# The null keys of the first wide attention: weights in token layout, and a second pair of matmuls once a sequence

## The chip, the cores and the metric

The kernel runs on one NeuronCore of a Trainium2 chip. The time is device microseconds, the median of three executions. A core has TensorE (PE, with its weight loads shown as PEld), VectorE (DVE), ScalarE (ACT), GpSimd (POOL) and SyncE (SP, which issues DMAs). Each works off its own instruction queue in order; they wait for each other by semaphores.

## What is computed

Four transformer layers in a row on 16 sequences of 256 tokens and 128 features, in float32. The change touches the first layer's attention only, with 16 heads of 64, ALiBi, a causal mask, normalized queries and keys, and two learned null keys and null values per head that every token sees:

```python
nkv = null_kv.reshape(HEADS, NUM_NULL_KV, 2, DIM_HEAD)
k = jnp.concatenate([nk, k], axis=2)        # nk, nv: the two null keys and values of each head
v = jnp.concatenate([nv, v], axis=2)
q = _l2norm(q) * q_scale
k = _l2norm(k) * k_scale
sim = jnp.einsum('bhid,bhjd->bhij', q, k) * ATTN_SCALE + alibi, causal mask
attn = jax.nn.softmax(sim, axis=-1)
out = jnp.einsum('bhij,bhjd->bhid', attn, v)
return out.transpose(0, 2, 1, 3).reshape(b, n, HEADS * DIM_HEAD) @ w_out
```

The input of the attention is normalized twice (a layer norm outside, one inside), so each sequence needs two means and inverse deviations for each half of 128 tokens. The result is added to `x`, which stays in SBUF as `XR` through the whole kernel.

## The kernel before

Eight stages run one after the other; each is a class with one method per engine (`pe`, `act`, `dve`, `pool`, `sp`). The first, `Wide` with `kind == 0`, is the first attention. Its work is cut into **units** of one sequence `b` and four heads `u`, 64 in all, numbered g = 4b + u, and one **prep** per sequence (layer norms, transpose of the tokens `zT`, scores of the null keys `sn`). A unit has 23 parts k = 0 to 22, a prep 9. The function `ticks` lays them on a common time line: a unit begins every 4 ticks, so in one tick five or six units are at parts that differ by 4. Within a tick the parts are sorted by `rank`; parts of equal rank stand in the order in which they began, older ones first. This list, `self.order`, is the queue of PE, ScalarE and VectorE; GpSimd has its own, `pool_order`, sorted by `pool_rank`, which here is the same.

The parts of a unit (`self.tk`): `qk` (k = 0, 1), queries and keys in token layout by three fp32r matmuls each (`mm3`, high and low halves); ScalarE squares (`sqr`) and copies (`raw`) them; VectorE sums the squares (`ss`, k = 1, 2); GpSimd takes the power -0.5 and scales `raw` (k = 3, semaphore `unitq`); PE turns them (`turn`, k = 6, 7), VectorE makes the low halves `QL` and `KL`; `mx` (k = 9, 10), row maxima of the scores, which PE computes two units ahead together with `st`; `v` (12); `mT` (15), the maxima `nm` transposed; `st` (17, 18), transposed scores, exponentiated by ScalarE into `P`; `pv` (20), weighted values and the sums `sm`; `sT` (21), the sums transposed and inverted (`rs`); `out` (22), the output product `Y` in two PSUM tiles, scaled by VectorE into `T` and added to `XR` by GpSimd in four operations (`pool_sum`).

PSUM has eight banks that the stage takes in turn (`self.G`, `K.ps.take`): who takes a bank waits until its former content has been read. The score part takes its four banks before its first instruction, the masks (`mk`).

The null keys, before: VectorE computes their scores and biases with four small operations and a reduction (`dve_null`, line 820 on, at k = 8). ScalarE exponentiates them (line 626), GpSimd lays the weights, split in a high and a low half, into `pn` (lines 925 to 928, k = 12). PE transposes both halves of `pn` in `mT` behind the `nm` transposes, ScalarE copies them out as `pnT` (line 634), and `pe_pv` starts its accumulation with two matmuls against `nvs` (null values) and one against `nvo` (ones, for the sums). `dve_nvs` builds both from three loads through the staging buffers before the first unit.

The inverse deviations (`pool_rstd`, two GpSimd operations for each of two halves) are made in the tick of the part that needs the statistics: prep k = 0 and k = 2; VectorE makes `z` in k = 2 and k = 4, PE turns it at k = 6.

The lines at which the rows below stand are those of the helpers where a helper records: 2578 to 2580 are `mm3`, 2583 is `acc`, 2586 is `tr` (transpose), 2592 and 2594 the statistics, 2599 and 2601 `pool_rstd`, 2607 `z`, 891 `pool_sum`, 912 the power and 917 the scaling of `raw`.

## Time and profile before

| | us |
|---|---|
| median of 3 runs | 2607.7 (2597.29 to 2611.27) |
| the profiled execution | 2604.87 |
| its span | 2603.1 |
| first wide attention, from the first `nm` transposes to the last sum | 65.6 to 839.7 |

In the lines of the time line each row is a start in us, a duration in us, the engine, the line of the kernel, the operation, output and inputs, and a count where like instructions were merged; a row of the windows has its length and then the busy us (and instructions) of PE, PEld, DVE, ACT and POOL, the granted clock, the DMA share and GB/s; in square brackets stands how long the engine had nothing to do before it and who ended that. A matmul's duration includes its way through the array, so the distance from one start to the next tells what it costs PE.

### The profile page before, as it was taken

Reading aid. Unit: us, or ns where it says so; the run is one execution under the profiler, and the core shown is the slowest. Engines: PE = TensorE matmul, PEld = TensorE weight load, DVE = VectorE, ACT = ScalarE, POOL = GpSimd, SP = SyncE. Lnnn points to the kernel's source line nnn. Section 1 sums busy time; section 2 is a strip of 40 time slices with the busy share of each in tenths; the row PEclk is TensorE's granted clock in tenths of the full one; section 3 lists DMA queues with packets and bytes.
Section 4 is the critical chain, followed back from the end, with each engine's and each line's share of the span. In section 5 each row is a group of like instructions: output and inputs, shape, how many; then the busy total and the mean of one; then the engine's idle time right before and its main releaser. Section 6 shows DMA issues by size and latency. Waiting matters only on the chain. (4 is left out here: it accounts for less than half of the span.)

```text
span 2603.1 us, 62284 instructions
## 1 busy us (share of the span) xinstructions
PE 2382.6 (92%) x23977; PEld 1851.5 (71%) x23977; DVE 1684.1 (65%) x4424; ACT 1477.2 (57%) x3068; POOL 1575.3 (61%) x2498
## 2 busy tenths in 40 slices
PE   3999999999999879988999999999999958788897
PEld 3888888888887546656777787777778747455555
DVE  4677777777675357774544467777777622577676
ACT  3666666666665457765444466666666523466665
POOL 4678777777785354443433267777777721666664
PEclk9999999999999979999999999999999979899999
DMA  5960000000000010000000000000000045000000
GB/s 201 328 209 2 2 2 2 2 2 2 2 2 2 1 45 2 2 2 12 21 1 1 3 2 6 6 6 4 6 6 5 5 124 184 17 10 8 8 4 33
DMA packets 23111, 83.10 MB, mean 32 GB/s; under 512 B 4097, under 2 KB 11010, under 8 KB 21794
## 3 DMA queue, kind: packets, MB, share of 16 engines
q1 hardware_dynamic: 19666, 71.90, 8.6%
q0 software_dynamic: 3152, 7.21, 0.9%
q8 instruction: 193, 3.16, 0.5%
q14 instruction: 100, 0.82, 0.1%
HBM read 71.89 MB, written 46.79 MB: 46 GB/s over the span
## 5 line engine op out<-in xcount | busy, mean ns | idle before, releaser
L891 POOL TENSOR_TENSOR XR<-XR,T 128x256 f32<-128x256 f32 x512 | 376.5, 735 | 152.9 <-DVE T L770 122.7
L645 ACT ACTIVATE P<-ps 128x384 f32<-128x384 f32 (+1 forms) x512 | 250.6, 541 | 180.0 <-PE ps L2583 178.6
L2583 PE MATMUL ps<-P,V 128*64 128x256 f32 (+3 forms) x4096 | 332.8, 346 | 9.9 <-DVE O L1377 7.9
L1361 DVE TENSOR_REDUCE bm<-ps 128x3 f32<-128x384 f32 x512 | 260.2, 550 | 110.5 <-PE ps L2583 109.5
L2583 PEld LDWEIGHTS ps<-P,V 128*64 128x64 f32 (+1 forms) x4096 | 185.7, 123 | 131.0 <-issue 34.3
L1296 ACT ACTIVATE P<-ps 128x768 f32<-128x768 f32 x256 | 207.7, 811 | 97.6 <-PE ps L2583 96.7
L781 DVE TENSOR_REDUCE sm<-ps 128x2 f32<-128x512 f32 (+1 forms) x256 | 130.8, 553 | 181.0 <-PE ps L2583 180.9
L1461 POOL TENSOR_SCALAR_AFFINE_SELECT P<-P 128x512 f32<-128x512 f32 x256 | 162.6, 635 | 119.2 <-ACT P L1296 116.5
L904 POOL TENSOR_TENSOR PS<-P 128x256 f32<-128x256 f32 x256 | 181.6, 735 | 70.5 <-ACT P L645 70.1
L2583 PE MATMUL ps<-mk,identb 128*128 128x256 bf16 (+1 forms) x1024 | 204.9, 293 | 14.4 <-DVE bm L1361 12.2
L912 POOL TENSOR_TENSOR ss<-ss,nhalf 128x16 f32<-128x16 f32 x64 | 187.7, 2933 | 5.3
L770 DVE TENSOR_TENSOR T<-ps,rs 128x512 f32<-128x512 f32 x256 | 163.9, 682 | 9.7 <-PE ps L2583 8.3
L2578 PE MATMUL ps<-wA,zT 128*128 128x256 f32 (+1 forms) x544 | 168.9, 311 | 1.3 <-issue 1.3
L2583 PE MATMUL ps<-QH,KH 64*128 64x256 f32 (+1 forms) x1024 | 163.1, 314 | 1.0 <-ACT MT L632 0.9
L757 DVE TENSOR_REDUCE nm<-ps 128x2 fp32r<-128x512 f32 x256 | 161.9, 676 | 2.6 <-PE ps L2583 2.6
L653 ACT ACTIVATE OT<-ps 128x512 f32<-128x512 f32 x128 | 76.5, 598 | 153.0 <-PE ps L2583 153.0
L2601 POOL TENSOR_TENSOR stat<-stat,nhalf 128x1 f32<-128x1 f32 x256 | 147.2, 575 | 21.3
L2579 PE MATMUL ps<-wA,zT 128*128 128x256 f32 (+1 forms) x544 | 154.1, 284 | 0.0
L1668 POOL TENSOR_TENSOR hr<-hf,hr 128x512 fp32r<-128x512 f32 x48 | 62.0, 1292 | 150.5 <-DVE hr L1657 138.5
L2580 PE MATMUL ps<-wA,zT 128*128 128x256 f32 (+1 forms) x544 | 153.0, 282 | 0.0
L2583 PE MATMUL ps<-QH,KL 64*128 64x256 f32 (+1 forms) x1024 | 144.9, 279 | 0.0
L2583 PE MATMUL ps<-MT,KB 64*128 64x256 f32 (+1 forms) x1024 | 144.7, 278 | 0.0
(309 smaller groups left out, 7007.3 us busy)
## 6 DMA issues: line engine op xcount, KB each, us to landing
rows_i<-in_zero SPq DMA_DIRECT2D x16, 1208.0 KB, 31.2
rows_o<-in_zero SPq DMA_DIRECT2D x16, 1208.0 KB, 80.6
w<-in_m_w SPq DMA_DIRECT2D x23, 578.0 KB, 4.0
zt<-rows_i SPq DMA_DIRECT2D x23, 128.0 KB, 3.3
rows_o<-yo POOLq DMA_DIRECT2D x23, 128.0 KB, 3.9
stg<-in_t_w SPq DMA_DIRECT2D x11, 256.0 KB, 2.7
XR<-in_x SPq DMA_DIRECT2D x4, 512.0 KB, 8.6
out<-XR SPq DMA_DIRECT2D x8, 256.0 KB, 2.0
```

The costliest lines, as they stand in the source:

```text
L645: e.activation(self.P[at % 6][:, :], K.ps.ap("st", s, g, h)[:, 0:self.w], ACT.Exp, bias=0.0, scale=1.0 if kind == 0 else 0.125).then_inc(K ...
L757: e.tensor_reduce(nm[:, :, 64 * par + n], ps[:, :].rearrange("p (t c) -> p t c", t=2), X, ALU.max, negate=True).then_inc(K.ps.out_of("mx", ...
L770: e.tensor_tensor(self.T[g % 2][:, par], K.ps.ap("Y", s, g, par)[:, :].rearrange("p (a t c) -> p a t c", a=2, t=2), r[:, par].unsqueeze(3) ...
L891: p = po.e.tensor_tensor(x, x, self.T[g % 2][:, par, pr], ALU.add)
L904: po.e.tensor_tensor(self.PS[g % 2][:, h, :], P[:, 0:256], P[:, 256:512], ALU.add).then_inc(self.halved, 1)
L912: d = po.step(e.tensor_tensor(ss[:, 32:48], ss[:, 16:32], K.nhalf[:, 0:16], ALU.pow))
L1296: e.activation(self.P[(2 * g + n) % 6][:, :, 0:384], K.ps.ap("st", s, g, n)[:, :, 0:384], ACT.Exp, bias=0.0, scale=self.scale).then_inc(K. ...
L1361: e.tensor_reduce(bm[:, h, :], K.ps.ap("mx", s, g, h)[:, 0:384].rearrange("p (a c) -> p a c", c=128), X, ALU.max, negate=True).then_inc(K. ...
L1461: e.affine_select(own, own, [[0, 4], [1, 128]], ALU.is_ge, 0.0, base=0, channel_multiplier=-1).then_inc(self.masked, 1)
L2578: self.te.matmul(o, L[0], R[0], start=start, stop=False)
L2579: self.te.matmul(o, L[1], R[0], start=False, stop=False)
L2583: return self.te.matmul(o, l, r, start=start, stop=True, skip_group_check=True)
```

## The change

Three things change in this stage.

1. The null keys' weights stay in token layout. GpSimd makes the scores (`pool_null`, two operations behind the norm at k = 3), VectorE keeps only the reduction of `dve_null`. GpSimd adds the two weights of each head (k = 12, `pnull`); VectorE adds this to the transposed sums ahead of the reciprocal. At k = 22 GpSimd multiplies the weights by `rs` into a `pn` of [128, 64] for the whole sequence (`shared`). The transposes of `pn` in `mT` and the three matmuls ahead of `pv` are gone.
2. Once a sequence a new item "null" with two parts: PE transposes `pn`, ScalarE copies it out; PE multiplies it by `nvw` (null values times the output weights, [64, 256]), ScalarE copies the result out as `ny`, GpSimd adds it to `XR` (`nulled`). Its ranks are 3 and 0.5, its GpSimd rank is 8. `nvw` is made once by eight fp32 matmuls (`pe_nvw`) and two ScalarE copies at k = 8 of the first unit, from one load, which replaces the three loads and `dve_nvs`. The stage is done when the last `nulled` is counted.
3. Order: GpSimd makes the deviations one part later (k = 1, 3) with rank 6, behind the unit work of the tick, and `pool_sum` one part later (k = 23, rank 7). VectorE gets its own order, `dve_order`, in which prep parts other than the transpose have rank 6. A unit has 24 parts.

```diff
@@ -139,7 +139,7 @@
         self.K, self.s, self.kind = K, s, kind
         self.causal = kind == 0
         if kind == 0:
-            first, last, unit = 8, 9, 23
+            first, last, unit = 8, 9, 24
             self.tk = {"qk": 0, "turn": 6, "mx": 9, "v": 12, "mT": 15, "st": 17, "pv": 20, "sT": 21, "out": 22}
...
+            if kind == 0:
+                items.append((16 * b + first + 12 + unit, 2, "null", (b,), 2))
...
+        self.dve_order = [w for w in ticks(items, self.dve_rank) if not self.is_early(*w)]
...
+        return (self.nulled, b + 1) if self.kind == 0 else (self.summed, 4 * b + 4)
...
+        if name == "null":
+            return 3 if k == 0 else 0.5
         if name != "unit":
             return 5 if name == "behind" else 1
...
         if self.kind == 2 and name == "unit":
             return 0 if self.part("st", k - 1) is not None else 2
+        if name == "unit" and k == self.tk["out"] + 1:
+            return 7
+        if name == "null":
+            return 8
+        if self.kind == 0 and name == "prep":
+            return 6
         return self.rank(name, k)
...
+    def dve_rank(self, name, k):
+
+        return 6 if self.kind == 0 and name == "prep" and k != self.zT_at else self.rank(name, k)
...
+            elif name == "null":
+                self.pe_null(pe, *a, k)
             elif name == "unit":
+                if self.kind == 0 and a == (0, 0) and k == 8:
+                    self.pe_nvw(pe)
                 self.pe_unit(pe, *a, k)
+
+    def pe_nvw(self, pe):
+
+        K, n = self.K, self.nvs_at
+        ps = K.ps.take(pe, self.G, "nvw")
+        K.staged(pe, n)
+        for j in range(8):
+            p = pe.e.matmul(ps[0:64, 0:128], K.stg[n % 2][:, 64 * j:64 * j + 64], K.wO[:, 128 * j:128 * j + 128],
+                            start=j == 0, stop=j == 7)
+        p.then_inc(K.ps.full_of("nvw"), 1)
+
+    def pe_null(self, pe, b, k):
+
+        K, s = self.K, self.s
+        if k == 0:
+            ps = K.ps.take(pe, self.G, "pnT", s, b)
+            pe.wait_ge(self.shared, 4 * b + 4)
+            K.tr(ps[0:64, 0:128], self.pn[b % 2][:, :]).then_inc(K.ps.full_of("pnT", s, b), 1)
+        if k == 1:
+            ps = K.ps.take(pe, self.G, "nul", s, b)
+            pe.wait_ge(self.nvs_in, 1)
+            pe.wait_ge(*K.ps.read("nvw"))
+            pe.wait_ge(*K.ps.read("pnT", s, b))
+            K.acc(ps[:, 0:256], self.pnT[b % 2][:, :], self.nvw[:, :], start=True).then_inc(K.ps.full_of("nul", s, b), 1)
 
...
@@ -373,10 +420,6 @@
                     pe.wait_ge(*K.ps.read("mx", s, g, h))
             for i in range(2):
                 p = K.tr(ps[:, 128 * i:128 * i + 128], fv(nm[:, i, :]))
-            if kind == 0:
-                pe.wait_ge(self.pnull, g + 1)
-                for i in range(2):
-                    p = K.tr(ps[0:96, 256 + 128 * i:384 + 128 * i], fv(self.pn[g % 2][:, i, :]))
             p.then_inc(K.ps.full_of("mT", s, g), 1)
...
-        if kind == 0:
-            pe.wait_ge(self.nvs_in, 4)
-            pe.wait_ge(*K.ps.read("mT", s, g))
-            for pr in range(2):
-                c = 256 * u + 128 * pr
-                K.acc(pv[:, 256 * pr:256 * pr + 256], self.nvs[:, 0, c:c + 128], self.pnT[g % 2][:, :], start=pr == 0)
-            K.acc(sm[:, 0:256], self.nvo[:, 4 * u:4 * u + 4, :].rearrange("p h c -> p (h c)"), self.pnT[g % 2][:, :],
-                  start=True)
         pe.wait_ge(*K.ps.read("v", s, g))
...
-                              P[2 * pr + par][:, c:c + w], start=kind == 2 and kt == 0 and pr == 0)
+                              P[2 * pr + par][:, c:c + w], start=kt == 0 and pr == 0)
...
-                    p = K.acc(sm[32 * h:32 * h + 32, q:q + w], self.one[:, 0:32], P[h][:, c:c + w])
+                    p = K.acc(sm[32 * h:32 * h + 32, q:q + w], self.one[:, 0:32], P[h][:, c:c + w], start=kt == 0)
...
+            elif name == "null":
+                if k == 0:
+                    b = a[0]
+                    if b >= 2:
+                        ac.wait_ge(*self.K.ps.filled("nul", self.s, b - 2))
+                    ac.wait_ge(*self.K.ps.filled("pnT", self.s, b))
+                    ac.e.activation(self.pnT[b % 2][:, :], self.K.ps.ap("pnT", self.s, b)[0:64, 0:128], ACT.Copy).then_inc(
+                        self.K.ps.out_of("pnT", self.s, b), 1)
+                if k == 1:
+                    b = a[0]
+                    if b >= 2:
+                        ac.wait_ge(self.nulled, b - 1)
+                    ac.wait_ge(*self.K.ps.filled("nul", self.s, b))
+                    ac.e.activation(self.ny[b % 2][:, :], self.K.ps.ap("nul", self.s, b)[:, 0:256], ACT.Copy).then_inc(
+                        self.K.ps.out_of("nul", self.s, b), 1)
             elif name == "unit":
                 if a == (0, 0) and k == 2:
                     self.act_kb(ac)
+                if self.kind == 0 and a == (0, 0) and k == 8:
+                    self.act_nvw(ac)
...
+    def act_nvw(self, ac):
+
+        K = self.K
+        ac.wait_ge(self.nv_zero, 1)
+        ac.wait_ge(*K.ps.filled("nvw"))
+        for t in range(2):
+            r = slice(32 * t, 32 * t + 32)
+            i = ac.e.activation(self.nvw[r, 128 * t:128 * t + 128], K.ps.ap("nvw")[r, 0:128], ACT.Copy)
+            i.then_inc(*((K.ps.out_of("nvw"), 1) if t else (self.nvs_in, 1)))
...
-            i = e.activation(self.MT[g % 2][:, :], ps[:, 0:256], ACT.Copy)
-            if kind == 0:
-                i = e.activation(self.pnT[g % 2][:, :], ps[0:96, 256:512], ACT.Copy)
-            i.then_inc(K.ps.out_of("mT", s, g), 1)
+            e.activation(self.MT[g % 2][:, :], ps[:, 0:256], ACT.Copy).then_inc(K.ps.out_of("mT", s, g), 1)
...
-        for name, a, k in self.order:
+        for name, a, k in self.dve_order:
...
-                if self.kind == 0 and a == (0, 0) and k == 0:
-                    self.dve_nvs(dv)
                 self.dve_unit(dv, *a, k)
...
         if self.part("sT", k) is not None:
+            rs, sums = self.rs[g % 2], K.ps.ap("sT", s, g)[:, 0:256].rearrange("p (a c) -> p a c", c=32)[:, :, 0]
+            if kind == 0:
+                if g >= 2:
+                    dv.wait_ge(self.shared, g - 1)
+                dv.wait_ge(self.pnull, g + 1)
             dv.wait_ge(*K.ps.filled("sT", s, g))
-            e.reciprocal(self.rs[g % 2][:, :], K.ps.ap("sT", s, g)[:, 0:256].rearrange("p (a c) -> p a c", c=32)[:, :, 0]
-                         ).then_inc(K.ps.out_of("sT", s, g), 1)
+            if kind == 0:
+                dv.after(dv.step(e.tensor_tensor(rs[:, :], sums, self.sm[g % 4][:, 48:56], ALU.add)))
+            e.reciprocal(rs[:, :], rs[:, :] if kind == 0 else sums).then_inc(K.ps.out_of("sT", s, g), 1)
...
-    def dve_nvs(self, dv):
-
-        K, e, v = self.K, dv.e, self.nvs
-        for n, (a, b) in enumerate(((0, 512), (512, 1024), (1024, 1040))):
...
     def dve_null(self, dv, b, u):
 
 
-        K, s, g, e, ss, sm = self.K, self.s, 4 * b + u, dv.e, self.ss[(4 * b + u) % 4], self.sm[(4 * b + u) % 4]
-        rq = ss[:, 32:40].rearrange("p (t a r) -> p t r a", t=2, a=2).unsqueeze(4)
-        snr = self.sn[b % 2][:, :].rearrange("p (t h n) -> p t h n", t=2, n=2)[:, :, 4 * u:4 * u + 4, :].rearrange(
-            "p t (a r) n -> p t r a n", a=2)
-        sn = sm[:, 16:32].rearrange("p (t r a n) -> p t r a n", t=2, r=2, a=2)
-        nb = K.pc("nbias", 8 * u, 8).rearrange("p (a r n) -> p r a n", a=2, r=2)
-        dv.wait_ge(*K.ps.read("sn", s, b))
-        dv.wait_ge(self.unitq, 2 * g + 1)
-        if g >= 4:
-            dv.wait_ge(self.rec, g - 3)
-        for t in range(2):
-            d = dv.step(e.tensor_tensor(sn[:, t], snr[:, t], rq[:, t].to_broadcast([128, 2, 2, 2]), ALU.mult))
-        dv.after(d)
-        for t in range(2):
-            d = dv.step(e.tensor_tensor(sn[:, t], sn[:, t], nb, ALU.add))
-        dv.after(d)
+        g, e, sm = 4 * b + u, dv.e, self.sm[(4 * b + u) % 4]
+        dv.wait_ge(self.scored, g + 1)
         e.tensor_reduce(sm[:, 8:16], sm[:, 16:32].rearrange("p (a n) -> p a n", n=2), X, ALU.max, negate=True).then_inc(
             self.snl, 1)
...
         if self.kind == 0:
-            for pn in self.pn:
-                e.memset(fv(pn[:, :, :]), 0.0).then_inc(K.pn_in, 1)
+            e.memset(self.nvw[:, :], 0.0).then_inc(self.nv_zero, 1)
         for name, a, k in self.pool_order:
             if name == "prep":
                 n = K.nb[s] + (4 if self.kind == 0 else 2) * a[0]
-                if k == 0 or (k == 2 and self.kind == 0):
+                if self.kind == 0 and k in (1, 3) and not self.is_early(name, a, k - 1):
                     for i in range(2):
-                        K.pool_rstd(po, n + k + i)
+                        K.pool_rstd(po, n + k - 1 + i)
+                if self.kind == 2 and k == 0:
+                    for i in range(2):
+                        K.pool_rstd(po, n + i)
                 if k == 3 and self.kind == 2:
                     self.pool_bias(po, a[0])
...
+            elif name == "null" and k == 1:
+                b = a[0]
+                xs = K.XR[:, 2 * b:2 * b + 2, :].rearrange("p t c -> p (t c)")
+                po.wait_ge(self.summed, 4 * b + 4)
+                po.wait_ge(*K.ps.read("nul", s, b))
+                e.tensor_tensor(xs, xs, self.ny[b % 2][:, :], ALU.add).then_inc(self.nulled, 1)
             elif name == "unit":
                 if self.kind == 0:
                     self.pool_unit(po, 4 * a[0] + a[1], k)
                 elif self.part("st", k - 1) is not None:
                     self.pool_halves(po, 4 * a[0] + a[1], k - 1 - self.tk["st"])
-                if k == self.tk["out"] + (1 if self.kind == 2 else 0):
+                if k == self.tk["out"] + 1:
                     self.pool_sum(po, *a)
             elif name == "load":
...
+    def pool_null(self, po, g):
+
+        K, s, b, u, e, ss, sm = self.K, self.s, g // 4, g % 4, po.e, self.ss[g % 4], self.sm[g % 4]
+        rq = ss[:, 32:40].rearrange("p (t h) -> p t h", t=2).unsqueeze(3).to_broadcast([128, 2, 4, 2])
+        snr = self.sn[b % 2][:, :].rearrange("p (t h n) -> p t h n", t=2, n=2)[:, :, 4 * u:4 * u + 4, :]
+        sn = sm[:, 16:32].rearrange("p (t h n) -> p t h n", t=2, n=2)
+        nb = K.pc("nbias", 8 * u, 8).rearrange("p (h n) -> p h n", n=2).unsqueeze(1).to_broadcast([128, 2, 4, 2])
+        po.wait_ge(*K.ps.read("sn", s, b))
+        if g >= 4:
+            po.wait_ge(self.rec, g - 3)
+        po.after(po.step(e.tensor_tensor(sn, snr, rq, ALU.mult)))
+        e.tensor_tensor(sn, sn, nb, ALU.add).then_inc(self.scored, 1)
+
...
+            self.pool_null(po, g)
         if k == self.tk["mx"] + 3:
-            sm, pn = self.sm[g % 4], self.pn[g % 2]
+            sm = self.sm[g % 4]
             po.wait_ge(self.rec, g + 1)
-            if g >= 2:
-                po.wait_ge(*K.ps.filled("mT", s, g - 2))
-            po.wait_ge(K.pn_in, 2)
-            s6 = sm[:, 32:48].rearrange("p (t a) -> p t a", t=2)
-            d = po.step(e.tensor_copy(pn[:, :, 0:8], s6))
-            e.tensor_copy(pn[:, :, 64:72], s6)
-            po.after(d)
-            e.tensor_tensor(pn[:, :, 32:40], s6, fv(pn[:, :, 0:8]), ALU.subtract).then_inc(self.pnull, 1)
+            ex = sm[:, 32:48].rearrange("p (a n) -> p a n", n=2)
+            e.tensor_tensor(sm[:, 48:56], ex[:, :, 0], ex[:, :, 1], ALU.add).then_inc(self.pnull, 1)
+        if k == self.tk["out"]:
+            b, u = g // 4, g % 4
+            sm, ex = self.sm[g % 4], self.sm[g % 4][:, 32:48].rearrange("p (t h n) -> p t h n", t=2, n=2)
+            if b >= 2 and u == 0:
+                po.wait_ge(*K.ps.filled("pnT", s, b - 2))
+            po.wait_ge(*K.ps.read("sT", s, g))
+            e.tensor_tensor(
+                self.pn[b % 2][:, :].rearrange("p (t h n) -> p t h n", t=2, n=2)[:, :, 4 * u:4 * u + 4, :], ex,
+                self.rs[g % 2][:, :].rearrange("p (t h) -> p t h", t=2).unsqueeze(3).to_broadcast([128, 2, 4, 2]),
+                ALU.mult).then_inc(self.shared, 1)
...
-            for n, (a, b) in enumerate(((0, 512), (512, 1024), (1024, 1040))):
-                n += self.nvs_at
-                K.sp_stage(sp, n, K.stg[n % 2][0:96, 0:b - a], K.t["nvs"][:, a:b])
             for c in range(5):
                 n, w = self.kb_at + c, 512 if c < 4 else 128
                 K.sp_stage(sp, n, K.stg[n % 2][:, 0:w], K.t["kb0"][:, 512 * c:512 * c + w])
+            K.sp_stage(sp, self.nvs_at, K.stg[self.nvs_at % 2][:, :], K.t["nvs"])
```

## Rows read from the trace of the kernel before

**Rows 1.** The page, busy time of each engine, its share of the span, instructions.

```profile
PE 2382.6 (92%) x23977; PEld 1851.5 (71%) x23977; DVE 1684.1 (65%) x4424; ACT 1477.2 (57%) x3068; POOL 1575.3 (61%) x2498
```

**Rows 2.** The windows: one unit, one sequence; busy us of each engine, clock, DMA.

```profile
429.15:440.87 11.72, 11.72 (x142) 9.97 (x141) 8.66 (x25) 7.40 (x16) 9.63 (x15) 1.00 0.01 1
404.84:453.21 48.37, 48.37 (x567) 40.84 (x566) 34.95 (x91) 30.28 (x66) 37.72 (x53) 1.00 0.01 2
```

**Rows 3.** The waits of 62 to 880 us: total us, times, longest.

```profile
POOL XR L891 <- DVE T L770: 122.7, 49, 6.7
PEld ps L2586 <- POOL pn L928: 3.9, 16, 0.8
```

**Rows 4.** The time line of PE, from the second turn of a unit's inputs to its sums.

```profile
413.73 0.38 PE L2586 MATMUL ps<-ident,S 128*128 128x128 f32 x2
413.95 0.60 PE L2583 MATMUL ps<-mk,identb 128*128 128x256 bf16 x4
417.65 0.38 PE L2586 MATMUL ps<-ident,pn 128*96 128x128 f32 x2
417.87 0.60 PE L2586 MATMUL ps<-ident,raw 128*128 128x128 f32 x4
418.22 0.49 PE L2583 MATMUL ps<-pnT,nvs 96*128 96x256 f32 x2
418.55 0.28 PE L2583 MATMUL ps<-pnT,nvo 96*128 96x256 f32 x1
418.76 1.52 PE L2583 MATMUL ps<-P,V 128*64 128x256 f32 x16
```

**Rows 5.** The same time line, around a first half of `qk`, and ScalarE beside it.

```profile
422.39 0.28 PE L2580 MATMUL ps<-wA,zT 128*128 128x256 f32 x1
422.51 0.61 PE L2583 MATMUL ps<-mk,identb 128*128 128x256 bf16 x4
410.23 0.22 ACT L583 ACTIVATE sn<-ps 128x64 f32<-128x64 f32 x1
421.13 0.38 ACT L659 ACTIVATE S<-ps 128x256 f32<-128x256 f32 x1 [0.21 <-PE ps L2583]
...
422.76 0.60 ACT L596 ACTIVATE sqr<-ps 128x512 f32<-128x512 f32 x1 [0.17 <-PE ps L2580]
423.26 0.59 ACT L597 ACTIVATE raw<-ps 128x512 f32<-128x512 f32 x1
```

**Rows 6.** The time line of GpSimd in the same sequence.

```profile
430.59 3.17 POOL L891 TENSOR_TENSOR XR<-XR,T 128x256 f32<-128x256 f32 x4 [2.75 <-DVE T L770]
434.07 2.93 POOL L912 TENSOR_TENSOR ss<-ss,nhalf 128x16 f32<-128x16 f32 x1
437.08 2.05 POOL L917 TENSOR_TENSOR raw<-raw,ss 128x512 f32<-128x512 f32 x2
439.67 0.23 POOL L2599 TENSOR_SCALAR stat<-stat 128x1 f32<-128x1 f32 x1
440.86 0.57 POOL L2601 TENSOR_TENSOR stat<-stat,nhalf 128x1 f32<-128x1 f32 x1
```

**Rows 7.** The time line of VectorE, with one row of PE (446.06).

```profile
429.17 0.68 DVE L726 TENSOR_REDUCE ss<-sqr 128x8 f32<-128x512 f32 x1
441.54 0.35 DVE L2607 TENSOR_SCALAR z<-XR,stat 128x128 f32<-128x128 f32 x1 [0.32 <-POOL stat L2601]
445.17 0.74 DVE L734 SCALAR_TENSOR_TENSOR KL<-ps,par,KH 128x512 fp32r<-128x512 f32 x1
446.06 0.60 PE L2583 MATMUL ps<-mk,identb 128*128 128x256 bf16 x4
448.27 1.29 DVE L781 TENSOR_REDUCE sm<-ps 128x2 f32<-128x512 f32 x2 [0.45 <-PE ps L2583]
```

**Rows 8.** The time line at the start (PE) and at the end (GpSimd) of the stage.

```profile
64.71 1.09 PE L2586 MATMUL ps<-ident,raw 128*128 128x128 f32 x4 [2.51 <-POOL raw L917]
836.48 3.19 POOL L891 TENSOR_TENSOR XR<-XR,T 128x256 f32<-128x256 f32 x4 [1.67 <-DVE T L770]
```

51 lines of the change are left out of this document (20 added, 31 removed).

## The prediction

> **What bounds the kernel now.** I read the page first: TensorE is busy for 92% of the span, no other engine for more than 65% [rows 1]. The stretches of the first wide attention, second: four units (one sequence) take 48.37 us there, PE has no empty stretch, the granted clock is 1.00, and GpSimd is the next engine with 37.7 us, VectorE 35.0, ScalarE 30.3 [rows 2]. The waits, third: GpSimd's largest wait in this stage is for VectorE's `T` (122.7 us), and the only wait of PE's weight loads for another engine that recurs is the one for the null weights `pn`, 3.9 us in all [rows 3]. So the stage's length is what PE's queue issues; anything taken out of it counts 64 times, and any new wait of PE counts in full.
>
> An adjacency in the time line misleads here: a producer and a PE instruction that stand side by side often belong to different units. The null weights and maxima that PE transposes come from the unit's part several ticks back, so these have microseconds in hand. Where the slack is small has to be read from the order of the ticks.
>
> **What PE loses, per unit.** Two transposes of `pn` (417.65 to 417.87, 0.22 us) go. The two `nvs` matmuls and the `nvo` one run from 418.22 to the first `P,V` at 418.76, 0.54 us [rows 4]. With them gone the raw transposes, whose fourth starts three steps of 0.11 behind 417.87, at 418.20, are followed by `P,V` directly. The same kind of step, from a 128-column transpose to the next group, takes 0.11 us from the second transpose of `S` to the masks (413.73 to 413.95 for two) [rows 4]. I get 418.76 - 418.20 - 0.11 = 0.45, and 0.22 + 0.45 = 0.67. Lower bound: only the array time goes, two transposes at 0.11 and three matmuls of 256 columns at the 0.12 us that the last `wA,zT` takes to the masks [rows 5], 0.58; upper bound: the two stretches whole, 0.76. Times 64: 42.9 us (37 to 49). The wait for `pn` goes with them, 3.9 us [rows 3].
>
> The page "TensorE: Matmul & The Clock Gate" of the Trainium skill, section "Back-to-back issue gap", gives N/2.4 + 2.5 ns from one matmul to the next at the full clock. That is 0.11 us for 256 columns, which the trace bears out (0.12), but 0.056 for 128, where the transposes show 0.11. By the page alone the five instructions would be worth 0.44 us a unit, 28 us in all, and the forecast below would turn into 9 us slower than before.
>
> **What PE gains: the null pair.** Once a sequence PE transposes the four units' shares (rank 3: last in its tick, behind the `qk` matmuls of the newest unit) and then multiplies by `nvw` (rank 0.5: first in the next tick). Nothing stands between the two on PE, and between them ScalarE has to copy the transposed weights out; on ScalarE that copy is queued behind `sqr` and `raw` of the same `qk`. From the rows: last `qk` matmul starts at 422.39, masks at 422.51; ScalarE's second copy starts at 423.26 and its successor can start 0.5 later (as `raw` starts 0.5 after `sqr`), at 423.76 [rows 5]. A copy of 128 columns lies between the 64 columns of `sn` (0.22) and the 256 of `S` (0.38) [rows 5]: 0.28. So PE goes on at 424.1. The product is fp32 of 256 columns: `P,V` needs 1.52 us for sixteen passes, eight of 256 and eight of 128 side by side in pairs [rows 4], so 0.25 at most for one pass of 256; I take 0.46 for the two. The masks start at 424.56 instead of 422.51: 2.05 us. Bounds: 0.6 if the copy is hidden (transpose and product alone), 2.6 if the weight load of the product waits as well. All that is queued on PE behind it (scores, and through them both reductions) is late with it. Fourteen sequences have a `qk` in that tick, the last two have only the copy of V (about 1.3): 31.3 us.
>
> **GpSimd.** Per unit it loses three small operations and gets four (two for the null scores, one sum, one product), each taken at the 0.2 of the ones that go, plus the add of `ny` once a sequence at the 0.79 of one of the four parts of `XR` (3.17 for four) [rows 6]. Its sum falls from work behind a wait to work without one: `pool_sum` no longer sits at the tick in which `T` is made, where it idled 2.75 us [rows 6], but behind the next unit's norm. A unit is then 5.4 (norm) + 0.5 + 3.2 + 0.4 = 9.5 us, a sequence 38 + 3.5 (four deviations) + 0.8 = 42.3 against 47.9 of PE: 88%, not the bound. The norm's result has more time in hand than before.
>
> **The deviations and VectorE.** VectorE loses four small operations and gets one in front of the reciprocal; with 35 of 48 us it isn't the bound, this is worth nothing by itself. Its order decides. Let N be the start of the two `nm` transposes, 440.87 in the unit with the first norm. (a) `z` (k = 2) and its statistics now stand behind `QL` but still ahead of `KL`; the wait of 0.32 for the deviation goes, since GpSimd makes it two ticks earlier. `KL` ended at 445.91 and PE's masks, which take its bank, began at 446.06 [rows 7], 0.11 later than they would have by 0.12 from the last matmul. In the new kernel `KL` ends at N + 4.72, PE needs it at N + 4.41 (5.08 - 0.67), plus the 0.15 from VectorE to PE: a wait of 0.46, where it was 0.11. Added: 0.35, times 16 = 5.6 us (0 to 10). (b) `z` (k = 4) waits for deviations that GpSimd now makes behind the norm. The sum of squares ends at N + 0.7 (429.17 + 0.68 against 429.15 [rows 2, 7]), the power starts 0.35 later, the norm ends at N + 6.1 by the rows of 434.07 and 437.08, the null scores at 6.6, the two deviations (439.67 to 441.43 for two) at N + 7.5 and 8.4 [rows 6]. VectorE stands at `z` until N + 8.85 with the sums of squares, the first maxima and the reciprocal queued behind it. The first maxima were taken at 448.27, N + 7.4 [rows 7], and would now be ready at N + 7.0: 1.9 us late. Who waits: the eight banks go round, and these banks are taken next by the transposes of `z` and by `Y`, some 3.3 us of PE work later (PE runs scores, their maxima and the second half in between). The two maxima (1.29 [rows 7]) end at N + 10.1, PE wants the bank at about N + 10.4. I charge 0.1 a sequence, 1.6 us (0 to 26).
>
> **Start and end.** `nvw` is eight fp32 matmuls on PE before the first maxima; PE is starved by GpSimd there (it waits 2.51 us for `raw` at 64.7 [rows 8]), so this is hidden, but `z` of sequence 1 now waits for a deviation behind a norm: 1.3 us (-2 to 3). The removed conversion of `nvs` on VectorE was beside ScalarE's work: nothing. At the end GpSimd adds `ny` after the last sum (836.48, four in 3.19 us [rows 8]): 0.8. SP issues three transfers fewer and one more, all ahead of the large fills: nothing.
>
> **The sum**, against the profiled execution (2604.9 us; span 2603.1): -42.9 - 3.9 + 31.3 + 5.6 + 1.6 + 1.3 + 0.8 = -6.2, so 2598.7. The median of the runs shown is 2.8 above that execution (2607.7): forecast 2601 us, its own range 2592 to 2613.
>
> **Rivals.** *B, the null pair is hidden*: PE reaches the product when the weights are out, because ScalarE comes to them earlier than I read. For it: ScalarE is idle a third of the time. Against: every `sqr` waits for PE, so it is never ahead of it. Price: 14 x 1.45 = 20 us less, 2581. *C, only array time is saved*: the step from the transposes to `P,V` keeps the 0.21 that it has behind `nvo` (418.55 to 418.76 [rows 4]), so 0.58 a unit: 5.8 us more, 2607, no change. *D, the other side*: VectorE at `z` (k = 4). My slack there is 0.1 to 0.3 us; each microsecond by which GpSimd's deviations come later (its null scores with broadcast operands slower than 0.25 each, a norm that starts later) stands on PE once a sequence. With 1.6 us more it is 16 x 1.6 = 26 us, 2627; it decides against the change from 0.4 us on. For it: GpSimd is in nobody's shadow here, a chain of power, product and two deviations without a gap; against: the rest of VectorE's queue in that tick is short.
>
> **Chances.** Forecast 0.48, B 0.17, C 0.20, D 0.15. What one measurement can tell from no change is about 0.5%, 13 us. Faster by more: most of B and an edge of the forecast, 0.29; slower: most of D and an edge of C, 0.17; the same 0.54. The range 2579 to 2624 holds the forecast and C, and reaches to B's value and D's.
>
> **What would show it.** Three of four units at some 11.05 us between `nm` transposes, from 11.72. Once a sequence a PE wait of 1.5 us for ScalarE's `pnT` ahead of the product: if it is under 0.5, B. GpSimd's wait for `T` gone from first place. VectorE's `z` waiting 3 to 4 us for `stat` once a sequence, and a PE wait behind it: over 0.5 us is D. It is wrong if a sequence takes under 46.5 or over 49 us.

## The result: slower by 0.47%, and the page after

| | us |
|---|---|
| changed kernel, median of 10 runs | 2616.97 (2614.89 to 2624.24) |
| kernel before, beside it on the same chip, 10 runs | 2607.48 (2596.80 to 2612.61) |
| ratio to the kernel before, 95% interval | 1.0047 (1.0033 to 1.0062) |
| profiled execution and its span | 2624.24; 2622.6 (before 2604.87; 2603.1) |
| first wide attention, from the first to the last `nm` transposes | 67.2 to 834.5 (before 65.6 to 823.5) |

The forecast was 2601 us, 0.25% under the median shown before. The time lies in the range given (2579 to 2624), outside the forecast's own one (2592 to 2613), and the sign is wrong. The profiled execution is the longest of its ten: the stage with the change and what follows up to `beff` (the start of the second wide attention) take 13.6 us more than before (`beff` from 1478.3 to 1491.9 us), which is what the ratio says (0.47% is 12.2 us). The rest of its 19.5 us more arises in stages that the change doesn't touch. So 13.6 is the number to explain, against the -6.2 of the sum.

The page of the changed kernel, busy time and TensorE's granted clock in 40 slices; it answers to [rows 1]:

```profile
PE 2377.0 (91%) x23721; PEld 1833.5 (70%) x23721; DVE 1594.8 (61%) x4222; ACT 1471.5 (56%) x3038; POOL 1605.8 (61%) x2577
PEclk9999999999999969999999999999999979799999
```

256 instructions fewer on PE, 5.6 us less busy time, and yet slower: the page alone would have passed for a gain. The windows tell more. Here each row is one unit of the changed kernel, from its `nm` transposes to those of the next, two sequences one behind the other (columns as in [rows 2]: length, busy us of PE, PEld, DVE, ACT, POOL, granted clock, DMA):

```profile
348.60:360.87 12.27, 11.97 (x138) 9.69 (x137) 8.33 (x23) 7.62 (x16) 11.24 (x18) 1.00 0.01 2
360.87:372.69 11.82, 11.82 (x142) 10.05 (x141) 7.21 (x20) 7.36 (x16) 8.87 (x12) 1.00 0.01 1
372.69:386.09 13.40, 12.03 (x140) 9.74 (x139) 6.20 (x15) 7.68 (x17) 9.61 (x13) 1.00 0.01 1
386.09:397.25 11.16, 11.16 (x136) 9.39 (x135) 7.57 (x23) 7.15 (x15) 9.38 (x13) 1.00 0.01 2
...
421.70:436.62 14.92, 13.55 (x140) 11.17 (x139) 6.59 (x18) 7.68 (x17) 9.60 (x13) 0.89 0.00 1
```

The first unit holds the transposes of `z`, the second the projection for `sn`, the third the null pair, the fourth nothing extra. Before, the four took 12.34, 12.59, 11.72 and 11.72 (the last is the first line of [rows 2]). Three things are to be seen. The clean unit is 0.56 shorter, not 0.67. The third unit has 13.40 - 12.03 = 1.37 us in which PE is idle. And in the next sequence the same unit takes 14.92, with the same 1.37 us idle but 1.52 more busy for the same 140 matmuls, at a granted clock of 0.89 of full. Whole sequences, windows of the same kind:

```profile
348.60:397.25 48.65, 46.99 (x549) 38.86 (x548) 29.30 (x79) 29.81 (x64) 39.10 (x56) 1.00 0.01 2
...
496.45:546.64 50.19, 48.53 (x550) 40.31 (x549) 29.41 (x79) 29.81 (x64) 39.42 (x57) 0.97 0.01 2
546.64:595.28 48.64, 46.98 (x549) 38.85 (x548) 29.30 (x79) 29.80 (x64) 39.43 (x57) 1.00 0.01 2
```

From the third sequence on every second one shows the clock at 0.97 and 1.5 us more, six in all (they begin at 199, 298, 397, 496, 595 and 694 us). A sequence of 48.37 [rows 2] became one of 48.65 or of 50.2: even without the clock there would be no gain.

The time line of PE around the null pair, in the unit from 421.70 (it answers to [rows 5]; `pn` and `nvw` are the pair):

```profile
421.92 0.60 PE L2642 MATMUL ps<-ident,raw 128*128 128x128 f32 x4
422.45 1.52 PE L2639 MATMUL ps<-P,V 128*64 128x256 f32 x16
...
426.10 0.28 PE L2636 MATMUL ps<-wA,zT 128*128 128x256 f32 x1
426.21 0.27 PE L2642 MATMUL ps<-ident,pn 128*64 128x128 f32 x1
427.86 0.67 PE L2639 MATMUL ps<-nvw,pnT 64*128 64x256 f32 x2 [1.37 <-ACT pnT L587]
428.45 0.61 PE L2639 MATMUL ps<-mk,identb 128*128 128x256 bf16 x4
429.00 0.38 PE L2639 MATMUL ps<-QH,KH 64*128 64x256 f32 x2
...
432.06 0.41 PE L2636 MATMUL ps<-wA,zT 128*128 128x256 f32 x1
...
433.89 0.28 PE L2639 MATMUL ps<-QH,KL 64*128 64x256 f32 x2
```

From the last `qk` matmul to the masks it takes 2.35 us, where [rows 5] have 0.12: 2.23 for the pair. From 1.7 us behind the pause on, the same kind of matmul lasts 0.41 instead of 0.28 us and starts 0.21 instead of 0.12 behind its forerunner, until 433. The window of exactly that stretch is at half of the full clock, 1.2 GHz:

```profile
429.60:433.00 3.40, 3.40 (x27) 3.18 (x24) 1.43 (x3) 0.87 (x2) 2.59 (x5) 0.51 0.02 5
```

The waits of 62 to 890 us, those that answer to [rows 3] and the new ones (total us, times, longest):

```profile
POOL ss L963 <- DVE ss L783: 95.6, 44, 4.5
DVE z L2663 <- POOL stat L2657: 65.8, 45, 4.2
PE ps L2639 <- ACT pnT L587: 20.0, 16, 1.4
POOL XR L931 <- DVE T L833: 9.2, 5, 2.6
PEld ps L2639 <- DVE sm L844: 5.6, 14, 0.4
```

GpSimd's wait for `T` fell from 122.7 us to 9.2 and that of the weight loads for `pn` is gone. GpSimd now waits for its sums of squares, which come from PE by way of two engines; that is idle time of an engine that isn't the bound.

VectorE at the second `z` (with one row of GpSimd and three of PE), where rival D had its place, and `KL`; they answer to [rows 6, 7]:

```profile
451.70 0.72 DVE L791 SCALAR_TENSOR_TENSOR KL<-ps,par,KH 128x512 fp32r<-128x512 f32 x1
452.19 0.28 PE L2636 MATMUL ps<-wA,zT 128*128 128x256 f32 x1
452.57 0.60 PE L2639 MATMUL ps<-mk,identb 128*128 128x256 bf16 x4
...
455.65 0.34 DVE L2663 TENSOR_SCALAR z<-z,stat 128x128 f32<-128x128 f32 x1 [3.15 <-POOL stat L2657]
455.82 0.59 POOL L2657 TENSOR_TENSOR stat<-stat,nhalf 128x1 f32<-128x1 f32 x1
457.13 1.27 DVE L844 TENSOR_REDUCE sm<-ps 128x2 f32<-128x512 f32 x2
458.46 1.16 PE L2639 MATMUL ps<-wO,OT 64*128 64x128 f32 x16 [0.16 <-DVE sm L844]
```

### The profile page after: what moved, and what is told of

It reads as the page before. It is cut to its first block and busy times, and to the rows that moved or that the text cites. A ratio compares the mean times of both kernels' runs of the same rounds, so it can differ in the third digit from the quotient of the medians.

```text
span 2622.6 us, 61622 instructions
## 1 busy us (share of the span) xinstructions
PE 2377.0 (91%) x23721; PEld 1833.5 (70%) x23721; DVE 1594.8 (61%) x4222; ACT 1471.5 (56%) x3038; POOL 1605.8 (61%) x2577
## 5 line engine op out<-in xcount | busy, mean ns | idle before, releaser
L2634 PE MATMUL ps<-wA,zT 128*128 128x256 f32 (+1 forms) x544 | 171.3, 315 | 1.4 <-issue 1.3
L2635 PE MATMUL ps<-wA,zT 128*128 128x256 f32 (+1 forms) x544 | 155.4, 286 | 0.0
L2636 PE MATMUL ps<-wA,zT 128*128 128x256 f32 (+1 forms) x544 | 155.0, 285 | 0.0
L2639 PE MATMUL ps<-QL,KH 64*128 64x256 f32 (+1 forms) x1024 | 145.4, 279 | 0.0
```

Source lines behind the costliest of these rows:

```text
L2634: self.te.matmul(o, L[0], R[0], start=start, stop=False)
L2635: self.te.matmul(o, L[1], R[0], start=False, stop=False)
L2639: return self.te.matmul(o, l, r, start=start, stop=True, skip_group_check=True)
```

## The experiments

Two theories stood after the comparison. **Pause and clock**: the null pair leaves PE idle for 1.37 us, and this pause both costs its own length and brings the clock down behind it. **Late z** (D): the deviations behind the norm hold VectorE, and PE behind it. A third question was how much of the unit's saving is really there. All ratios are to the kernel before on the same chip; the changed kernel stands at 1.0047.

**e1, the product moved behind the work of its tick.** The only edit, in `rank`:

```diff
-            return 3 if k == 0 else 0.5
+            return 3 if k == 0 else 4
```

> The product with nvw keeps its tick but goes from the first to the last place in it (rank 4 instead of 0.5), on PE and ScalarE; GpSimd's order is untouched. Theory (the null pair leaves PE idle for about 1.4 us once a sequence, and every second time the granted clock falls to half for 3.4 us, which costs 1.5 us more): the wait for pnT goes from 20 us to under 1, no half-clock stretch is left between 240 and 740 us, and the kernel is 16 x 1.6 + 7 x 1.5 = 36 us faster than the changed kernel, about 2582 us, 1% under the kernel before. Rival (the stall is elsewhere given back, as in VectorE's z or in a bank that the pair holds): at most 10 us faster, 2606 or more.

Measured: 2580.97 us, ratio 0.9933 (0.9915 to 0.9952). This is the fastest kernel of the case that computes the whole result, 1.1% under the changed one and 0.7% under the one before. Its null unit and a whole sequence, as windows, and PE around the pair:

```profile
409.43:421.42 11.99, 11.99 (x140) 9.77 (x139) 6.51 (x18) 7.57 (x17) 9.54 (x13) 1.00 0.01 1
337.85:385.06 47.21, 46.96 (x550) 38.91 (x549) 29.30 (x79) 29.68 (x64) 39.04 (x56) 1.00 0.01 2
```

```profile
413.94 0.27 PE L2642 MATMUL ps<-ident,pn 128*64 128x128 f32 x1
414.05 0.60 PE L2639 MATMUL ps<-mk,identb 128*128 128x256 bf16 x4
...
417.29 0.70 PE L2639 MATMUL ps<-nvw,pnT 64*128 64x256 f32 x2
417.92 0.61 PE L2639 MATMUL ps<-mk,identb 128*128 128x256 bf16 x4
```

The scores and the second half of `qk` stand between transpose and product, PE has no idle time in that unit, and the pair costs 11.99 - 11.16 = 0.83 us, 11.16 being the clean unit behind it. No sequence falls under clock 1.00. By parts: the null unit is shorter by 1.41 us (13.40 - 11.99) in thirteen sequences and by 0.86 in the last two that have a pause in this stage, where it is only 0.91 and 0.82 us, together 20.0 us, and 6 x 1.52 = 9.1 are the clock's. That makes 29.1; from the first to the last `nm` transposes the stage takes 738.5 us instead of 767.4, 28.9 less, and the ratios differ by 1.14%, 29.7 us.

**e2, the pause filled.** To part pause and clock, eleven matmuls without use run between transpose and product; the product still waits for the same copy:

```diff
         if k == 1:
             ps = K.ps.take(pe, self.G, "nul", s, b)
+            for i in range(11):
+                pe.e.matmul(ps[:, 256:512], K.wA[:, 0, 0:128], K.wA[:, 0, 1024:1280], start=True, stop=True)
```

> The changed kernel with eleven extra fp32r matmuls of 256 columns (results unused) between the transpose of the shares and the wait for pnT: PE is busy in what was the gap, the order is the same and nothing is faster by itself. Theory (half of the extra time in these sequences is the clock): the spacing of the nm transposes loses its 1.5 us in every second sequence, no half-clock stretch between 240 and 740 us, 7 x 1.5 = 10 us faster than the changed kernel, about 2607. Rival (the 1.5 us have another cause, the clock only follows): the same as the changed kernel or slower by the matmuls that reach over the wait (up to 0.2 x 16 = 3 us), 2617 to 2620.

Measured: 2599.06 us, ratio 0.9997 (0.9987 to 1.0007).

```profile
418.00:431.33 13.33, 13.33 (x151) 11.10 (x149) 6.51 (x18) 7.67 (x17) 9.59 (x13) 1.00 0.00 1
```

The unit is as long as in the changed kernel, but it never takes 14.92, and every sequence is at clock 1.00. Work for nothing made the kernel 0.50%, 13 us, faster. In the profiled executions the stage is 9.7 us shorter (757.7 us instead of 767.4 from the first to the last `nm` transposes), and 9.1 of these are the six falls of the changed kernel; what the ratio has beyond that isn't attributed.

**e11, the pause half filled.** Against e2:

```diff
-            for i in range(11):
+            for i in range(4):
```

> The changed kernel with four filler matmuls instead of the eleven of e2 between the transpose of the shares and the product: they cover about 0.5 to 0.9 of the 1.65 us; the product still starts when ScalarE's copy is out, so the sequence isn't longer by them. If the fall of the clock needs the full length of the pause, it is gone and the time is that of e2: 0.5% under the changed kernel, 1.000 of the kernel before. If any pause at this place makes it fall, the stretches at half clock remain and the ratio is 1.005.

Measured: 2608.42 us, ratio 1.0016 (1.0001 to 1.0030). The pause before the product is 0.81 us (0.80 to 0.90 in thirteen sequences):

```profile
423.27 0.70 PE L2641 MATMUL ps<-nvw,pnT 64*128 64x256 f32 x2 [0.81 <-ACT pnT L589]
```

All its sequences stand at clock 1.00 and 48.6 us, as in e2, and its last `nm` transposes come at 823.2 us (e2: 824.8). The time is 0.2% above e2's all the same; in the profiled executions that difference arises behind this stage, where up to `beff` PE is busy for 593.3 us instead of 585.0 with the same matmuls, at a granted clock of 0.95 instead of 0.96. What the clock does there isn't under the control of this edit. So the mechanism is borne out by the windows, the price by the ratio only in part.

**e8, the pause alone, in the kernel before.** PE waits once a sequence for a copy of ScalarE:

```diff
             elif name == "unit":
+                if self.kind == 0 and a[1] == 1 and k == 17 and a[0] + 1 < NSEQ:
+                    pe.wait_ge(*self.K.ps.read("qk", self.s, 4 * a[0] + 5, 0))
                 self.pe_unit(pe, *a, k)
```

> The kernel before with one added wait of PE once a sequence: ahead of the masks of the first score half in the tick of the null pair it waits until ScalarE has copied the newest qk half out (which the masks don't need). PE's queue, work and banks are those of the kernel before, only a gap of about 1.4 us is put in 15 times. Theory (such a gap is paid a second time by the granted clock in every second sequence): 15 x 1.4 + 7 x 1.5 = 31 us more, 1.012, half-clock stretches of 3.4 us some 97 us apart. Rival (the clock falls only together with what else the changed kernel does around the gap): 21 us more, 1.008, granted clock 1.00 throughout.

Measured: 2622.20 us, ratio 1.0089 (1.0069 to 1.0110). The pause is 1.24 us, fifteen times; the sequence grew by 1.4 us (48.37 to 49.77) and the clock did not fall once in the stage, where I had looked for it:

```profile
431.59 0.61 PE L2585 MATMUL ps<-mk,identb 128*128 128x256 bf16 x4 [1.24 <-ACT raw L599]
```

```profile
400.16:449.94 49.78, 48.54 (x566) 40.84 (x565) 35.02 (x91) 30.30 (x66) 37.75 (x52) 1.00 0.01 2
```

**e9, the same pause in all four units.** Against e8:

```diff
-                if self.kind == 0 and a[1] == 1 and k == 17 and a[0] + 1 < NSEQ:
-                    pe.wait_ge(*self.K.ps.read("qk", self.s, 4 * a[0] + 5, 0))
+                if self.kind == 0 and k == 17 and a[0] + 1 < NSEQ:
+                    pe.wait_ge(*self.K.ps.read("qk", self.s, 4 * a[0] + a[1] + 4, 0))
```

> The kernel before with the pause of e8 (PE waits for ScalarE's copy of the newest unit's raw, 1.4 us) in all four units of fifteen sequences, not in one. If the fall of the clock depends on how much PE idles overall, the granted clock now falls to half in this stage, many times. If it depends on something local to the null pair, there is no stretch at half clock here either, and the price is pauses alone: 60 x 1.4 = 84 us, about 2690 us, sequences of 54.0 us instead of 48.4.

Measured: 2685.85 us, ratio 1.0323 (1.0306 to 1.0340). The sixty pauses of 1.24 us and what follows them cost 83 us; a sequence takes 53.64. In two of the fifteen sequences the clock fell, once in each, directly behind one of the pauses:

```profile
372.00:427.17 55.17, 50.22 (x566) 42.27 (x565) 34.63 (x91) 30.26 (x66) 37.61 (x52) 0.97 0.00 1
427.17:480.81 53.64, 48.69 (x566) 40.83 (x565) 34.41 (x91) 30.26 (x66) 37.73 (x52) 1.00 0.01 2
```

Here PE is idle for 5 us of each sequence, three times as long as in the changed kernel, with a third of its falls. It isn't the idle time as a whole.

**e10, the pause with short units.** The kernel of e6 (below) with the pause of e8.

> The kernel without the null keys' matmuls on PE (e6, the null values are left out of the output) with the pause of e8 once a sequence. A pause is 1.4 us: sequences of 48.4 us instead of 47.0, 21 us more than e6 (2580), 2601. If the shorter units are what tips the clock together with a pause, stretches at half clock of 3.4 us appear every second sequence and a pair of sequences takes 1.5 us more: 12 us on top, 2613. If the clock goes by the length of the pause alone (1.4 here, 1.65 in the changed kernel), it stays at 2.4 GHz.

Measured: 2603.72 us, ratio 0.9994 (0.9981 to 1.0007), 0.7% above e6. Sequences of 48.44 us and clock 1.00:

```profile
345.02:393.46 48.44, 46.17 (x546) 38.48 (x545) 35.07 (x91) 29.23 (x62) 37.77 (x53) 1.00 0.01 2
```

The one fall between 100 us and the end of the loop stands in the unit at 98.5, where PE waits 0.89 and 1.03 us within 2 us for VectorE, not behind the inserted pause. Short units don't tip it.

**e12, the pause alone, longer.** e8, and ScalarE squares that half twice ahead of the copy:

```diff
+            i = e.activation(self.sqr[at % 3][:, :], K.ps.ap("qk", s, g, n)[:, :], ACT.Square)
+            if kind == 0 and g % 4 == 1 and g >= 5 and n == 0:
+                i.then_inc(self.twice, 1)
+                ac.wait_ge(self.twice, g // 4)
+                e.activation(self.sqr[at % 3][:, :], K.ps.ap("qk", s, g, n)[:, :], ACT.Square)
```

> The kernel before with the pause of e8 once a sequence, made longer: ScalarE squares the same half twice ahead of the raw copy for which PE waits. PE then idles some 1.8 to 2.1 us instead of 1.24, more than the 1.37 of the changed kernel, and everything else is as before. If the length of one pause makes the clock fall, there are now stretches at half clock in this stage in at least five of the fifteen sequences, 1.5 us each: sequences of 50.3 to 50.7 us and some above 51.5, 2632 us or more in all (1.011 to 1.016 of before). If the fall in the changed kernel comes from what stands around its pause (shorter units, the fp32 product), the granted clock stays at 1.00 here, and the time is that of the pauses alone, 2602 + 15 x 2.2 = 2635 at most.

Measured: 2648.50 us, ratio 1.0183 (1.0155 to 1.0210), above the range of both theories. The pause is 1.87 us; two sequences of the fifteen as windows:

```profile
442.14 0.61 PE L2590 MATMUL ps<-mk,identb 128*128 128x256 bf16 x4 [1.87 <-ACT raw L604]
```

```profile
356.66:410.08 53.42, 51.55 (x566) 43.34 (x565) 35.01 (x91) 30.87 (x67) 37.73 (x53) 0.94 0.01 2
...
565.77:616.19 50.42, 48.55 (x566) 40.86 (x565) 34.91 (x91) 30.86 (x67) 37.72 (x53) 1.00 0.01 2
```

Nine of fifteen sequences are under clock 1.00, two of them twice over (53.42, 3.0 us more), eleven falls in all. By parts, 15 x 2.05 for the pauses (50.42 - 48.37) and 11 x 1.5 for the clock are 47 us, which is the ratio. This settles what e8 left open: between e8 and e12 PE's own queue is the same and only the length of one pause differs (ScalarE has one square more in each sequence). Put in order of length, each kernel by its one profiled execution:

| kernel | pause, us | how many were followed by a fall of the clock |
|---|---|---|
| e1, e2 | none in the null unit | none |
| e11 | 0.81 | none of 13 |
| e8, e10 | 1.24, once a sequence | none of 30 |
| e9 | 1.24, four times | 2 of 60 |
| changed kernel; e3 | 1.37 | 6 of 13; 5 of 13 |
| e12 | 1.87 | 9 of 15 |

The kernel before has one such place too, at the end of its loop, with two pauses within 1.4 us:

```profile
768.31 0.63 PE L2586 MATMUL ps<-ident,raw 128*128 128x128 f32 x4 [1.17 <-POOL raw L917]
769.70 0.42 PE L2586 MATMUL ps<-ident,pn 128*96 128x128 f32 x2 [0.54 <-POOL pn L928]
743.26:795.37 52.11, 50.39 (x572) 42.59 (x571) 39.98 (x105) 31.16 (x67) 41.03 (x62) 0.97 0.01 2
```

From 770.20 to 773.61 us its granted clock is 0.51. So what the changed kernel does in six sequences stood once in the trace of the kernel before; two short pauses side by side can do it as well, though not always (e1 has 0.93 and 1.03 us within 2 us near the end of its loop, and no fall).

Each fall costs 1.5 us (14.92 - 13.40; 15.33 in e9's unit instead of 13.81). Why some pauses of one length are followed by it and others not stays open.

**e3, the old order of the deviations in the changed kernel.** GpSimd makes them at k = 0 and 2 with the old ranks, and VectorE's prep parts have theirs:

```diff
-        if self.kind == 0 and name == "prep":
-            return 6
...
-        return 6 if self.kind == 0 and name == "prep" and k != self.zT_at else self.rank(name, k)
+        return self.rank(name, k)
...
-                if self.kind == 0 and k in (1, 3) and not self.is_early(name, a, k - 1):
+                if self.kind == 0 and k in (0, 2):
...
-                        K.pool_rstd(po, n + k - 1 + i)
+                        K.pool_rstd(po, n + k + i)
```

> The changed kernel with the deviations and VectorE's prep parts where they were before (prep k = 0 and 2, rank 1, VectorE in the common order); the sum of GpSimd stays late. Theory: VectorE's wait at z for stat falls from 66 us to about 10, PE's waits for VectorE's maxima (some 8 us in 14 sequences with the weight loads) go, the unit with the z transposes takes 11.8 instead of 12.3: 0.5 x 16 = 8 us faster, about 2609. Rival (the late deviations paid for themselves by freeing GpSimd for the norm): PE waits for raw or KL instead, the same or slower, 2617 or more.

Measured: 2609.37 us, ratio 1.0048 (1.0032 to 1.0065), the same as the changed kernel. VectorE's wait for the deviations falls to a quarter, and PE waits for `KL` in its place:

```profile
DVE z L2661 <- POOL stat L2655: 15.5, 32, 0.8
PE ps L2637 <- DVE KL L789: 10.1, 15, 1.0
```

The `z` unit takes 12.40 where it took 12.27. The new order of the deviations is worth about 0.1 us a sequence (the late `pool_sum`, which this edit leaves in place, is e7), and D is out as the cause.

**e4, the edits of e1 and e3 together.**

> Both edits in one kernel: product last in its tick, deviations and VectorE's order as before. Theory: the gains add up, 36 + 8 = 44 us under the changed kernel, about 2573, 1.3% under the kernel before; sequence of 46.5 us. Rival: whichever of the two doesn't hold by itself is missing here too; if both hold alone but not together, 2582 or more, GpSimd at 88% of the time is the next bound.

Measured: 2586.21 us, ratio 0.9948 (0.9930 to 0.9966), no better than e1 (the intervals overlap): its sequences take 47.35 us, 0.14 more, and PE waits 10.0 us in 15 for `KL`.

**e5, e1 with VectorE making `z` one part later** (k = 3 and 5), so that it need not wait for GpSimd:

```diff
-        if k == 2:
+        if k == (3 if self.kind == 0 else 2):
...
-        if self.kind == 0 and k == 4:
+        if self.kind == 0 and k == 5:
```

> The late product (rank 4) and GpSimd as in the changed kernel, but VectorE's prep parts one tick later: first z with its statistics at k = 3 instead of 2, so behind KL, and second z at k = 5 instead of 4, so behind the first maxima, the sum of squares and the reciprocal of that tick. Theory (VectorE's order makes both PE waits: in the late-product kernel the one at z costs 0.45 us a sequence, with the old order KL costs 0.6): neither PE wait is left, the unit with the z transposes takes 11.8 us instead of 12.23, 16 x 0.4 = 6 us under the late-product kernel, 0.9907 of the kernel before. Rival: the z transposes now wait for the later second z themselves, the same 0.4 us at another place, 0.993 or more.

Measured: 2583.14 us, ratio 0.9941 (0.9923 to 0.9960), the same as e1. VectorE's wait falls from 68.6 us in e1 to 13.1, and PE now waits for `z` itself:

```profile
PE ps L2642 <- DVE z L2663: 17.4, 16, 5.7
DVE z L2663 <- POOL stat L2657: 13.1, 21, 2.4
```

The transposes of `z` come right behind it; there is no slack on that side either. In e1 that wait of PE was 9.6 us in two. The unit with `z` takes 12.22 us, in e1 12.23: the masks no longer wait for `KL`, and in their place the transposes of `z` wait 0.50. VectorE's 68.6 us of waiting cost PE 0.6 us a sequence at most (below), and taking them away moved that cost instead of removing it.

**e6, the saving by itself.** The kernel before without the null keys' two transposes and three matmuls on PE (the null values and their share of the sums are missing from the output; VectorE's and GpSimd's work stays):

```diff
         if kind == 0:
-            pe.wait_ge(self.pnull, g + 1)
-            for i in range(2):
-                p = K.tr(ps[0:96, 256 + 128 * i:384 + 128 * i], fv(self.pn[g % 2][:, i, :]))
...
-            for pr in range(2):
-                K.acc(pv[:, 256 * pr:256 * pr + 256], self.nvs[:, 0, c:c + 128], self.pnT[g % 2][:, :], start=pr == 0)
-            K.acc(sm[:, 0:256], self.nvo[...], self.pnT[g % 2][:, :], start=True)
...
-                i = e.activation(self.pnT[g % 2][:, :], ps[0:96, 256:512], ACT.Copy)
```

> The kernel before without the null keys' share on PE (the two transposes of pn, the two nvs and the nvo matmul and the copy of pnT are left out; the output lacks the null values, the sums lack the null weights). It measures the term of the sum that a unit saves, by itself. Theory by the trace of the changed kernel (the step from the raw transposes to P,V takes 0.20 us and not 0.11): clean units at 11.16 us, 64 x 0.56 + 4 for the waits for pn = 40 us less, 0.9847. Rival (the unit saving was 0.67 and the changed kernel lost a tenth elsewhere in every unit): 11.05, 47 us less, 0.982.

Measured: 2580.35 us, ratio 0.9923 (0.9905 to 0.9941), a gain of about half of what was expected. Two units of one sequence, the one with `z` and the clean one, and PE's wait:

```profile
332.53:345.46 12.93, 11.90 (x138) 9.73 (x137) 10.14 (x29) 7.56 (x16) 11.11 (x17) 1.00 0.01 1
...
368.43:379.56 11.13, 11.13 (x136) 9.35 (x135) 8.65 (x25) 7.14 (x15) 9.12 (x13) 1.00 0.01 1
```

```profile
PE ps L2569 <- DVE KL L720: 14.8, 15, 1.0
```

The clean unit is 0.58 shorter than before. But the unit with `z` is longer than before (12.93 against 12.34), since VectorE's `KL` doesn't keep up with a shorter unit: PE is idle there for 1.03. The whole sequence is 47.03, 1.34 less, not the 2.3 that four units promise. So with the old order and the old work of VectorE and GpSimd, even null keys that cost PE nothing bring about as much as e1 does with them (0.9933; the intervals overlap).

**e7, `pool_sum` one part later in the kernel before.**

```diff
-            first, last, unit = 8, 9, 23
+            first, last, unit = 8, 9, 24
...
+        if name == "unit" and k == self.tk["out"] + 1:
+            return 7
...
-                if k == self.tk["out"] + (1 if self.kind == 2 else 0):
+                if k == self.tk["out"] + 1:
```

> The kernel before with GpSimd's sum one part later (k = 23, rank 7: behind the next unit's norm), nothing else. Theory (GpSimd bounds nothing in this stage): the wait for T falls from 123 us to under 20, the norm is done 4 us sooner, PE is not faster: 3 us less at most (part of the waits for pn), ratio 0.999 to 1.001. Rival (the room that this makes carries a gain that the changed kernel used up): 0.996 or less.

Measured: 2595.78 us, ratio 0.9979 (0.9966 to 0.9992). GpSimd's wait for `T` falls to 17.7 us, the wait of PE for `pn` goes, and a sequence takes 48.07: 0.3 less, or 4.8 us for sixteen, more than the 3 us expected. Of the 0.3, 0.16 stands in the unit with the projection (12.57 to 12.41), where PE waited for `pn`, and 0.11 in the unit with `z` (12.34 to 12.23), where it waited for `KL`. That unit, without any wait of PE:

```profile
341.68:353.91 12.23, 12.23 (x144) 10.25 (x142) 9.20 (x31) 7.83 (x17) 10.16 (x15) 1.00 0.00 1
```

## Why the prediction was wrong

Each term of the sum against what the windows of the changed kernel and the experiments show:

| term | forecast | measured | difference |
|---|---|---|---|
| unit saving, 64 times | 0.67 | 0.56 | +7.0 |
| waits for `pn` | -3.9 | gone | 0 |
| null pair, 14 times | 2.05 | 2.24 | +2.7 |
| granted clock | not in the sum | 6 x 1.52 | +9.1 |
| `KL` and `z`, 16 times | 0.45 | 0.49 | +0.6 |
| end of the loop in the kernel before | not in the sum | -2.5 | -2.5 |
| start | +1.3 | +1.6 | +0.3 |

With the -6.2 of the forecast that makes +11.0, where the stage up to `beff` shows +13.6; 2.6 us remain unassigned. Part of them arises behind the last `nm` transposes, where PE is busy for 587.5 us up to `beff` instead of 584.9. The row on the end of the loop is the kernel before's own pauses and fall at 768 to 774 us: they make its fifteenth sequence 52.11 us long, 3.7 more than the others, where the changed kernel's takes 49.92, 1.3 more than the others without a fall.

**The unit.** The prediction took the two transposes (0.22, right) and 0.45 for the rest, for which the step from the last transpose to `P,V` had to be 0.11. After the change the second raw transposes start at 421.92 and `P,V` at 422.45: three steps of 0.11 and a last one of 0.20. The 0.21 that stood ahead of `P,V` in [rows 4] belongs to `P,V`, not to `nvo`; this is rival C's mechanism, at a little more than C's price (7.0 us instead of 5.8). The step that misled, from the transposes of `S` to the masks, leads to another kind of group. The clean unit is 11.16 against 11.05 forecast. The Trainium skill's rule cited in the prediction ("TensorE: Matmul & The Clock Gate", section "Back-to-back issue gap") would have made it 0.44 a unit; the same section calls that rule the gap of an isolated matmul and puts a stream of weight loads and matmuls of 128 columns at about 81 ns each. The transposes here take 0.11 us. The measured 0.56 lies just under the lower bound of 0.58 that the rows gave.

**The null pair.** This step held in kind and nearly in size: 1.37 us of PE's wait against the 1.5 foretold, 2.23 for the pair against 2.05. B is refuted. The product takes 0.59 from its start to the masks, not the 0.46 taken.

**The clock, the step that failed.** The prediction read "the granted clock is 1.00" as given for the stage and priced the pause at its length. The new wait of 1.37 us is the longest that recurs in this stage, and in six of the thirteen sequences that have it PE ran at 1.2 instead of 2.4 GHz for 3.4 us behind it. No case of mine held this, though the trace of the kernel before has such a fall at 770 us, behind pauses of 1.17 and 0.54. With 9.1 us it is the largest of the differences; the unit's 7.0 is the next, and neither alone turns -6.2 into +13.6. Without the 9.1 us the measured 13.6 would be 4.5, no change by the bound of 0.5%, and e2, the same pause filled, is at 0.9997. Experiments e2 and e11 show that shortening the pause removes the falls, e12 that lengthening it alone produces them.

**`KL` and `z`.** The unit with `z` took 12.34 before; less 0.56 that is 11.78, and it takes 12.27: 0.49. (Against e7, where it takes 12.23 without any wait of PE, it is 0.60.) The forecast charged 0.35 to `KL` and 0.1 to `z`; it is the other way round. `KL` ends at 452.42, and PE's masks (452.57) come 0.26 later than a step of 0.12 from the last matmul (452.19) would bring them, where it was 0.11 before: 0.15 is `KL`'s, and 0.34 is left for `z`, behind which VectorE stands for 3.15 us and its maxima reach PE 0.16 late. So D is there with 0.34 us, about a fifth of the 1.6 that it asked for.

**What the prediction said would show it.** A sequence over 49 us was to prove it wrong: every second one is. The wait for `T` gone, the wait of 3 to 4 us at `z`, and PE's wait for `pnT` are all there.

What the case was worth stands in one rank: the same change with the product behind the scores (e1) is at 0.9933 instead of 1.0047.

## To carry to other kernels

Of two dependent instructions of a saturated engine with another engine's copy between them, put at least one tick's independent work in between; compare the copy's end by the time line with where the second instruction stands in the queue. Price a new pause of TensorE twice, by its length and by what the granted clock may do behind it, also where the sequences that were looked at stand at full clock; search the whole stage of the old trace for a fall and for the pause ahead of it. And before a stage's saving is multiplied by its count, look for the engine that would be late next in each kind of unit (here VectorE at `KL`, already 0.11 us late before the change in one unit of four): it caps the gain, whatever is taken out.
